# A gate's activation from one ScalarE function, and one VectorE pass for the gated product instead of two, in the expert stage of a decoder layer

## What is computed

```python
scores = sigmoid(xt @ w_router.T)
topk_w, topk_i = top_k(scores, 2)
topk_w = topk_w / topk_w.sum(-1, keepdims=True)
gate = silu(einsum('th,eih->tei', xt, wg))          # 8 experts, 640 hidden units
up = einsum('th,eih->tei', xt, wu)
expert_out = einsum('tei,ehi->teh', gate * up, wd)
out = einsum('te,teh->th', comb, expert_out)
sgate = silu(einsum('th,jih->tji', xt, sg))         # 2 shared experts
sup = einsum('th,jih->tji', xt, su)
out = out + einsum('tji,jhi->th', sgate * sup, sd)
x = layernorm(x + out)
```

## Time and profile before

| | |
|---|---|
| Median of 3 timed runs | 883.74 us (883.25 to 884.34) |
| The profiled execution | 880.8 us |
| Its span, first to last instruction | 878.5 us |
| Mean granted TensorE clock | 0.935 |
| TensorE busy (matmuls) | 772.1 us, 88% |
| VectorE busy | 585.0 us, 67% |
| ScalarE busy | 512.3 us, 58% |
| GpSimd busy | 312.7 us, 36% |

### The profile page before, as it was taken

The page is one execution under the profiler, slowest core; times in us unless marked ns, Lnnn a source line. Parts: engine busy times, 40 slices in busy tenths (PEclk is TensorE's granted clock), DMA queues, the critical chain, the costliest instruction groups (busy, mean ns, idle before and its releaser), DMA issues. The chain is left out here.

```text
span 878.5 us, 19798 instructions
## 1 busy us (share of the span) xinstructions
PE 772.1 (88%) x7471; PEld 499.8 (57%) x7471; DVE 585.0 (67%) x1300; ACT 512.3 (58%) x941; POOL 312.7 (36%) x481
## 2 busy tenths in 40 slices
PE   2878888999999999998768989998999999999993
PEld 1335455555555555555434555566778778777662
DVE  2454677877787777776427988786656666565574
ACT  2344577787778777786423554554555555555443
POOL 3132344555555555555220276000222222222222
PEclk8577699999999999999659999999999999999998
DMA  8109000000000000000012578241232233222231
GB/s 239 61 22 275 1 2 2 2 1 2 2 2 3 1 2 2 1 3 1 1 31 92 163 229 265 101 138 37 45 49 47 46 49 50 43 45 48 48 110 60
DMA packets 38282, 50.99 MB, mean 58 GB/s; under 512 B 9265, under 2 KB 33073, under 8 KB 38193
## 3 DMA queue, kind: packets, MB, share of 16 engines
q1 hardware_dynamic: 31040, 40.39, 15.5%
q0 software_dynamic: 7152, 9.34, 6.5%
HBM read 31.04 MB, written 18.68 MB: 57 GB/s over the span
## 5 line engine op out<-in xcount | busy, mean ns | idle before, releaser
L1326 POOL DMA_INDIRECT acc<-y_sb,xin x39 | 60.5, 1552 | 223.1 <-ACT y_sb L1394 223.1
L1650 PE MATMUL ps<-wr,xr_hi 128*128 x624 | 129.3, 299 | 0.0
L675 DVE TENSOR_REDUCE c_qs<-ps 128x4 f16<-128x512 f32 x128 | 83.4, 692 | 37.3 <-PE ps L933 35.7
L1650 PE MATMUL ps<-xg_hi,wsh 128*128 128x512 f16 x320 | 103.4, 385 | 4.3 <-DVE xg_lo L1512 4.3
L675 DVE TENSOR_REDUCE a_qs<-ps 128x4 f16<-128x512 f32 x128 | 85.2, 690 | 24.2 <-PE ps L933 23.1
L508 ACT ACTIVATE a_pt<-ps 128x512 f32<-128x512 f32 x128 | 74.7, 595 | 41.9 <-PE ps L950 39.6
L1365 ACT ACTIVATE th<-ps 128x384 f32<-128x384 f32 (+1 forms) x118 | 57.2, 485 | 71.1 <-PE ps L1650 70.9
L1650 PE MATMUL ps<-wr,xr_lo 128*128 x312 | 93.4, 299 | 0.0
L1370 ACT ACTIVATE hs<-th 128x384 f16<-128x384 f32 x78 | 36.6, 470 | 78.2 <-DVE th L1522 78.2
L508 ACT ACTIVATE c_pt<-ps 128x512 f32<-128x512 f32 x128 | 69.8, 604 | 19.8 <-PE ps L950 19.5
L1519 DVE SCALAR_TENSOR_TENSOR th<-th,ps 128x384 f32<-128x384 f32 (+1 forms) x118 | 65.0, 550 | 22.8 <-ACT th L1365 22.5
(11 more groups left out here) (209 smaller groups left out, 1759.6 us busy)
## 6 DMA issues: line engine op xcount, KB each, us to landing
wst<-in_wx SPq DMA_DIRECT2D x30, 640.0 KB, 4.4
xs<-zero SPq DMA_DIRECT2D x1, 5031.0 KB, 23.2
xin<-xs SPq DMA_DIRECT2D x39, 129.0 KB, 2.1
acc<-x_row SPq DMA_DIRECT2D x4, 512.0 KB, 3.3
x_row<-acc SPq DMA_DIRECT2D x8, 256.0 KB, 5.6
out<-x_row SPq DMA_DIRECT2D x8, 256.0 KB, 2.1
x_row<-in_x SPq DMA_DIRECT2D x1, 1536.0 KB, 10.7
wst<-in_wqkvT SPq DMA_DIRECT2D x1, 768.0 KB, 4.6
```

Of the source, the lines that this page charges most:

```text
L675: dve.tensor_reduce(t.qs[:].rearrange("p (c i) s -> p c i s", i=NI)[:, c:c + 4, f % 4, USED], score_bank(t, "m", b, f).rearrange("p (j n) ...
L1326: pool.indirect_dma_start(acc, bass.IndirectOffsetOnAxis(ap=row, axis=0), y_sb[:, n % 2, :], None, compute_op=ALU.add).then_inc(f_acc, 16)
L1650: ins = pe.matmul(o, l[x], r[y], start=(first and n == 0), stop=(last and n == m - 1), skip_group_check=not (first and last))
```

## The change

ScalarE computes silu of the gate in place of tanh of half of it, at the same place in its list; VectorE's first pass, the semaphore `f_act` and the wait on it go, and its second pass has another constant. Uses of `tanh(...)` become `silu(...)` with the same arguments.

```diff
-            def tanh(h, k, n):
+            def silu(h, k, n):
...
-                act.activation(th[:, k % 2, 0:n], gate[:, k % 2, 0:n], ACT.Tanh, scale=0.5 / WSCALE
+                act.activation(th[:, k % 2, 0:n], gate[:, k % 2, 0:n], ACT.Silu, scale=1.0 / WSCALE
                                ).then_inc(f_th, 1)
...
                 t = th[:, k % 2, 0:n]
                 dve.wait_ge(f_th, h + 1)
-                dve.scalar_tensor_tensor(out=t, in0=t, scalar=1.0, in1=gate[:, k % 2, 0:n],
-                                         op0=ALU.add, op1=ALU.mult).then_inc(f_act, 1)
-                dve.wait_ge(f_act, h + 1)
-                dve.scalar_tensor_tensor(out=t, in0=t, scalar=0.5 / WSCALE ** 2, in1=up[:, k % 2, 0:n],
+                dve.scalar_tensor_tensor(out=t, in0=t, scalar=1.0 / WSCALE, in1=up[:, k % 2, 0:n],
                                          op0=ALU.mult, op1=ALU.mult).then_inc(f_hid, 1)
```

More of the change, by code:

```diff
@@ L1219, in experts @@
     f_up = sem("f_up")
-    f_th, f_act, f_hid = sem("f_th"), sem("f_act"), sem("f_hid")
+    f_th, f_hid = sem("f_th"), sem("f_hid")
     f_hhi, f_hlo = sem("f_hhi"), sem("f_hlo")
@@ L1374, in group @@
                     h = STEPS * g + s
-                    tanh(h, s, GT)
+                    silu(h, s, GT)
                     k = s - first_piece(g)
@@ L1407, in last_group @@
                 for s in range(STEPS):
-                    tanh(HL + s, s, GT)
+                    silu(HL + s, s, GT)
                     hidden_high(HL + s, s, ht_hi[:, s % 2, 0:GT])
@@ L1419, in unit @@
                     c0, c1 = HALVES[half]
-                    tanh(HR + 2 * n + half, half, (c1 - c0) * P)
+                    silu(HR + 2 * n + half, half, (c1 - c0) * P)
                     if half == 0 and k < TILES - 1:
```

## The result

The changed kernel takes 873.12 us (median of 4 runs, 872.48 to 873.48); the kernel before takes 883.5 us (4 runs, 880.99 to 884.34). The ratio is 0.9888, with a 95% interval of 0.9868 to 0.9907: 8 to 12 us faster. Of the forecast 875.0 us (871.8 to 879.3), the time lies in the range, and the gain, 9.9 us by the ratio, is 1.2 us above the 8.7 of the sum. One of the six executions of that set was a slow one, 2507.75 us, and is left out of its median.

A forecast was written before the change was run, and what follows sets the result against it. VectorE was taken to bound group 0, TensorE the routed tiles and last group. Gains of 4.6 + 1.4 + 0.6 + 1.4 + 0.7 = 8.7 us, taken from the 883.7 us median, gave 875.0 us (range 871.8 to 879.3).

The forecast's parts named there:

- group 1: Second group of the expert stage: stays at the pace of the weight buffers, gain 0.
- 3. first tile: First routed tile: TensorE's 1.5 us wait for the first gated half shortens, gain 0.6 us.
- 5. last step: Very end of the kernel: nothing covers the chain, so all that follows moves up, gain 0.7 us.
- 6. table load: Before the first activation: the new table load lies in ScalarE's 5.67 us idle stretch, cost 0.
- term 1: Group 0, where VectorE bounds the steps: removing its pass gains 4.6 us (3.8 to 5.6).
- term 4: Routed tiles after the first: earlier weighing of results ends two late tile loads, 1.4 us gained (bounds 0 and 2.6).
- term 2: Ends of groups 0 to 2: input's low part comes earlier; 0.7 us at each later two, 1.4 us gained.
- slow rival: Routed tiles: silu takes longer than tanh, each tile grows by D - 0.69 us; about 892 us, chance 0.03.
- weight-buffer rival: Group 0: the weight-buffer loop binds once VectorE does not; gain falls to 5.6 us, time 878.1, chance 0.20.
- More late tile loads: Routed tiles: term 4 gives nothing and two or three more stalls appear; about 880 us, chance 0.05.

## Why the prediction was right, point by point

The mechanism was right for group 0, the boundaries, the first tile and the last step: the pass is worth what lies on the chain into TensorE, not its 65 us. For the other tiles it was at best a part. The gains of the profiled pair, by the terms of the sum:

| term | forecast | measured |
|---|---|---|
| 1. group 0 | 4.6 | 4.46 to step 9, of which 2.10 was lost again at the end of the group |
| group 1 | 0 | 0.27 |
| 2. the two later boundaries | 1.4 | 0.72 + 0.73 |
| 3. first tile | 0.6 | 0.63 |
| 4. the other tiles | 1.4 | 3.24 |
| 5. last step | 0.7 | 0.70 |
| 6. table load | 0 | 0 |
| sum | 8.7 | 8.65 |

That the sum came out within 0.1 us is luck: 2.1 us that term 1 left out and 1.8 that term 4 had too little cancelled, and in the second profile of the same kernel the end of group 0 lost only 0.4.

**Term 1** was right up to step 9 and in all one-pass kernels alike (36.66 to 36.70 us; 41.15 to 41.20 with two passes). Its companion in term 2, "At the end of group 0 I count nothing more, because ScalarE is there held by a weight piece", named the right obstacle and stopped short: when the rest came earlier and the piece did not, the piece became what everything waited for, 0.4 us in one profile and 2.1 in the other, where the clock fell behind the wait. The input first in ScalarE's list removes it.

**Term 4** was sized too small, and its mechanism is not what the runs bear out. Its step "I take those 1.4 us as gone" came true (no wait for a tile load is left), but two profiles with two passes and the result at its old place have none either, so in part by chance. The upper bound of 2.6 was passed. The result moves 0.59 us and not 0.85. What the term lacked altogether are the pauses ahead of the down product, 2.5 us before and 0.5 after. Seven further profiles with one pass in the tiles and the usual gate have 215.20 to 216.24 us, four with two passes 217.21 to 218.53. Their means differ by 2.5 us, where this pair has 3.9 (both with the 0.63 of the first tile), so term 4 at some 2 us is typical. How a later gated half brings those pauses without a wait for `hs` stays open.

**The slow rival** fell with the first silu row, 597 ns. Its arithmetic was wrong as well, since "the slack is 0.69 us" was read from the last tile; in the middle of the stage the low part comes 0.35 us before TensorE wants it, not 0.12, and with one pass 0.94. An activation 0.91 us longer cost 2.5 us in the tiles and some 4 by the ratios, where 39 times D - 0.69 would have given 8.6. The Trainium skill (ScalarE: Activation LUTs, Step-by-step: what each stage is for) says that an element costs the same whatever the function; tanh 595, sigmoid 595 and silu 597 ns bear it out.

**The weight-buffer rival** describes something real, but not caused by the change: group 1 takes 37.6 us before and 37.3 after in the first pair, and up to 41 in others of either kind. Its spread, 36.79 to 40.97 us over all profiles, is a good part of what makes them differ. **More late tile loads** did not come: no profile with one pass in the tiles has a wait for one. **The table load** was covered as stated, and its 1283 ns is what the row of before has. The 2.66 us that the Trainium skill (ScalarE: Activation LUTs, What ACT_TABLE_LOAD costs) gives for a switch with its drain can't be seen here. The load starts 0.02 us after the copies, so no drain shows ahead of it, and what may follow it lies in the 4.30 us in which ScalarE waits for TensorE.

**The median.** The same gain was taken from the median as from the profiled execution. By the ratio the timed gain is 9.9 us against 8.65 in the expert stage of the profiled pair. Part of the distance is the choice of executions: the profiled one of the kernel before (880.8 us) lay below all its timed ones, and that of the changed kernel (873.48) was the longest of four. The intervals are too wide to say more.

## What to carry to other kernels

Ask of a pass that is taken away which wait of the busiest engine it feeds, stage by stage: here 65 us of VectorE's work was worth 9. The largest part, 4.5 us, was won in the 40 us where that engine bounded the step, and 0.4 to 2.1 of it was lost again behind a late piece. Then look at what is queued beside the chain on each engine and lands by DMA, since that becomes the late one, and put what the busiest engine waits for ahead of it in the list. Read a slack from a typical iteration, never from the first or the last.

## What the hardware showed that I had not expected

After a wait of TensorE of 2.5 us at the end of group 0, the granted clock of the next two windows (3 and 4 us) was 0.70 and 0.80 in one execution and 1.00 in another of the same kernel. In the first, its matmuls of 512 columns took 0.43 us each for 3.4 us and then 0.215 again, so they ran at the lower of the two levels (1.2 GHz) for that time, and the step took 8.50 instead of 6.80 us. Four more kernels have this wait, 2.4 to 2.5 us each time: two of them show the low clock (8.41 and 8.48 us) and two don't (6.78 and 6.84). The same happens at the first tile, after a wait of 1.50 us in both profiles of the changed kernel (7.12 us at a granted clock of 1.00, 8.80 with 0.69 behind the wait). So the clock can add 1.7 us to a stall of 2.5, or nothing; what decides between the two, no run here shows.
